# Axial attention on one core: scores interleaved as pairs of sequences, relative parts with sequences innermost, a second output bank, and another order of products

## What is computed

```
rel = arange(H)[:, None] - arange(H)[None, :] + H - 1
q_pos, k_pos, v_pos = pos_relative[:, rel]            # 4, 4 and 8 rows
qk = einsum('nhcp,nhci->nhpi', q, k)
qr = einsum('nhcp,cpi->nhpi', q, q_pos) * gate_qr
kr = einsum('nhcp,cpi->nhpi', k, k_pos) * gate_kr
att = bn(concat([qk, qr, kr])); att = att summed over the three parts
att = softmax(att, axis=-1)
att_v  = einsum('nhpi,nhci->nhcp', att, v * gate_v)
att_vp = einsum('nhpi,cpi->nhcp', att, v_pos * gate_v_pos)
z = bn(concat([att_v, att_vp])), summed over the two parts
```

## Time and profile before

| | before |
|---|---|
| median of 3 runs | 19744.31 us |
| the profiled execution | 19778.58 us, its span 19776.8 us |
| busy, whole span | PE 11295.5, DVE 10181.0, ACT 5464.1, POOL 9546.2 us |
| mean granted TensorE clock (share of 2.4 GHz) | 0.688 |
| attention stage | 2264 to 6536 us of the span |
| attention stage, busy | PE 3135.53, DVE 2030.81, ACT 1336.88, POOL 267.64 us |
| split_qk stage | 1540 to 2216 us of the span |

### The profile page before, as it was taken

One profiled execution on the slowest core, in us unless ns is written; L12 is line 12 of the kernel. 1 busy time (PEld: TensorE's weight loads), 2 busy tenths in 40 slices (PEclk: granted clock), 3 DMA queues, 4 the chain that ended last, 5 costly groups with the idle time before them and its releaser, 6 DMA issues. The chain is left out here.

```text
span 19776.8 us, 195767 instructions
## 1 busy us (share of the span) xinstructions
PE 11295.5 (57%) x62482; PEld 5033.8 (25%) x62482; DVE 10181.0 (51%) x14908; ACT 5464.1 (28%) x7509; POOL 9546.2 (48%) x8283
## 2 busy tenths in 40 slices
PE   5553477777777103332333233333347899999998
PEld 2551244444444001111111111111112233333333
DVE  4557544444444333443444344344432577777777
ACT  1114333333333000000000000000000477777776
POOL 0113200000000106886888688688820477777777
PEclk9555565656656556666656666666679999999999
DMA  4004322222222494335333533533333202021211
GB/s 95 27 27 99 61 36 39 37 37 39 37 39 36 143 194 110 94 95 131 95 94 96 130 95 94 131 94 94 94 88 71 43 20 47 20 45 22 43 22 30
DMA packets 1429876, 1407.11 MB, mean 71 GB/s; under 512 B 777265, under 2 KB 1170753, under 8 KB 1413761
## 3 DMA queue, kind: packets, MB, share of 16 engines
q1 hardware_dynamic: 1137088, 743.01, 18.5%
q0 software_dynamic: 221184, 604.27, 10.6%
q10 hardware_dynamic: 70976, 50.83, 0.8%
HBM read 1036.88 MB, written 276.84 MB: 66 GB/s over the span
## 5 line engine op out<-in xcount | busy, mean ns | idle before, releaser
L1374 POOL DMA_INDIRECT dc_g<-corners,dc_idx x4608 | 5287.7, 1148 | 1325.8 <-issue 1255.1
L1990 POOL TENSOR_TENSOR df_sq<-df_sq 128x512 f32<-128x512 f32 x1920 | 2519.3, 1324 | 1944.7 <-ACT df_sq L1938 1898.9
L1447 PE MATMUL dc_ps<-ident,dc_s 128*128 128x128 f32 x2560 | 673.8, 429 | 4339.5 <-DVE dc_s L1538 4323.9
L2085 DVE SCALAR_TENSOR_TENSOR df_pr<-df_pk,vecs,df_h 128x512 f32<-128x512 f32 x2880 | 2093.8, 742 | 610.6 <-PE df_pk L1879 343.3
L1530 DVE TENSOR_TENSOR dc_g<-dc_g,dc_wt 128x2304 f32<-128x2304 f32 x512 | 1308.9, 2556 | 1795.5 <-DMA dc_g<-corners,dc_idx 1795.4
L1938 ACT ACTIVATE df_sq<-df_pk,vecs 128x512 f32<-128x512 f32 x2880 | 1935.3, 685 | 978.6 <-DVE df_pr L2085 955.0
L748 POOL TENSOR_TENSOR at_md<-at_mt,at_own 64x512 bf16<-64x512 f32 x256 | 267.6, 1045 | 4013.8 <-DVE at_mt L938 4013.8
L920 DVE SCALAR_TENSOR_TENSOR at_x<-at_pq,hconst,at_x 128x512 f32<-128x512 f32 x1024 | 741.3, 745 | 2191.3 <-PE at_pq L785 1657.6
L1407 ACT ACTIVATE dc_st<-dc_ps 128x512 f32<-128x512 f32 x640 | 327.1, 609 | 4735.9 <-PE dc_ps L1447 4728.1
L1447 PEld LDWEIGHTS dc_ps<-ident,dc_s 128*128 128x128 f32 x2560 | 471.6, 218 | 4523.5 <-DVE dc_s L1538 3145.9
L1876 PE MATMUL df_pk<-df_t,df_wp 64*128 64x512 f32 x3840 | 1351.1, 640 | 210.4 <-ACT df_sq L1938 156.7
(11 more groups left out here) (271 smaller groups left out, 17474.2 us busy)
## 6 DMA issues: line engine op xcount, KB each, us to landing
df_h<-df_h SPq DMA_DIRECT2D x160, 512.0 KB, 7.1
dc_g<-corners,dc_idx POOLq DMA_INDIRECT x4608
corners<-dc_xt SPq DMA_DIRECT2D x16, 4160.0 KB
at_a<-y SPq DMA_DIRECT2D x192, 192.0 KB
dc_xp<-x SPq DMA_DIRECT2D x8, 4096.0 KB
cv_xp<-x SPq DMA_DIRECT2D x8, 4096.0 KB, 52.5
y<-sp_p SPq DMA_DIRECT2D x128, 192.0 KB, 2.8
y<-sp_p SPq DMA_DIRECT2D x64, 384.0 KB, 4.3
```

The lines of the kernel that those rows point to most:

```text
L1374: nc.gpsimd.indirect_dma_start(gt[:, r, k, :, :].rearrange("p a c -> p (a c)"), None, image, bass.IndirectOffsetOnAxis(ap=idx[:, s, r, k:k ...
L1447: i = nc.tensor.transpose(ps[:, j, 128 * r:128 * r + 128], sm[:, r % 2, 128 * j:128 * j + 128], env.ident[:, :])
L1990: nc.gpsimd.tensor_tensor(a, a, sq[:, (KK * n + other) % RING, :], ALU.add).then_inc(nadded, 1)
L2085: nc.vector.scalar_tensor_tensor(out=rows(pr[:, j % RING, :]), in0=rows(pk[:, j % BANKS, :]), scalar=env.vecs[:, bias:bias + 1], in1=shift ...
```

## The change

All of it lies in split_qk and attention.

- X becomes `[nh pair, p, nh of the pair]`: two nh are interleaved, so that for each position two floats lie side by side. `qk` writes every second float of its bank, `times_v` reads every second float of X, and `times_vpos` reads pairs of floats.
- `y2` and `at_a` are stored with position parity e first, then position, then the 8 sequences innermost. A relative matmul now covers positions p and p + 1 (p even), the second copy of `at_rel` is shifted by 1 instead of 64, and the matmul reads runs of 8 bf16. split_qk's second scale reads `sp_z` with stride to write this order.
- `at_pvv` has two banks; the transposed maxima lose their own bank `at_ps` and go into a bank of `at_pt`. `times_v` takes bank q % 2, `times_vpos` alternates.
- The exponential is taken in two halves (128 x 1024 each).
- TensorE's order: the products with v stand between the spreads, the next group's first `qk` comes ahead of the relative matmuls, and these are spread over all four groups, two of them already in group 0 ahead of `times_vpos`.

The diff, cut to its core:

```diff
@@ split_qk, VectorE
-                                halves = lambda v: v.rearrange("c (w e h) -> c e w h", w=8, e=2) if a else v
+                                from_z = z[:, s, :].rearrange("c (w h e) -> c e h w", w=8, e=2) if a else z[:, s, :]
...
@@ attention
-        a = sb("at_a", [128, 2, 2, HEADS, NSEQ, H // 2], BF16)
+        a = sb("at_a", [128, 2, 2, HEADS, H // 2, NSEQ], BF16)
-        X = sb("at_x", [128, 2, NH, H])
+        X = sb("at_x", [128, 2, NH // 2, H, 2])
-        pq, ptt, prr, pvv, pss = pp("at_pq", 2), pp("at_pt", 2), pp("at_prr", 2), pp("at_pvv", 1), pp("at_ps", 1)
+        pq, ptt, prr, pvv = pp("at_pq", 2), pp("at_pt", 2), pp("at_prr", 2), pp("at_pvv", 2)
@@ qk
-                        last = nc.tensor.matmul(pq[:, t % 2, 128 * e:128 * e + 128], kb[96:120, s, nh // NSEQ, c],
+                        last = nc.tensor.matmul(pq[:, t % 2, :].rearrange("p (n b e) -> p n b e", n=2, e=2)[:, e // 2, :, e % 2], kb[96:120, s, nh // NSEQ, c],
@@ transposed_maxima
-                    pe.wait_ge(mt_out, u)
-                nc.tensor.matmul(pss[0:64, 0, 0:128], mx[:, q % 2, :], env.ident[:, :], start=True, stop=True).then_inc(mt_done, 1)
+                    pe.wait_ge(subbed, 4 * u - 1)
+                nc.tensor.matmul(ptt[0:64, q % 2, 0:128], mx[:, q % 2, :], env.ident[:, :], start=True, stop=True).then_inc(mt_done, 1)
@@ times_v
-                                            X[:, s, nh, :], start=True, stop=True, tile_position=(0, 32 * j))
+                                            X[:, s, nh // 2, :, nh % 2], start=True, stop=True, tile_position=(0, 32 * j))
@@ times_vpos
-                                                X[:, s, :, p], start=True, stop=True, tile_position=(0, 32 * j))
+                                                X[:, s, :, p, :], start=True, stop=True, tile_position=(0, 32 * j))
@@ relative
-                    p = 4 * r + i
+                    p = 8 * r + 2 * i
-                                            a[0:96, s, :, :, :, p].rearrange("c e h n -> c e (h n)"), start=True, stop=True)
+                                            a[0:96, s, :, :, p // 2, :].rearrange("c e h n -> c (e h) n"), start=True, stop=True)
@@ TensorE, work
-            RELS = {1: ((0, 1, 2), (3, 4)), 2: ((5, 6, 7), (8, 9)), 3: ((10, 11, 12), (13, 14, 15))}
+            RELS = {0: ((0, 1),), 1: ((2, 3), (4, 5, 6)), 2: ((7,), (8, 9, 10, 11)), 3: ((12,), (13, 14, 15))}
...
+                    spread_next(0)
+                    spread_next(1)
                     qk(k, s, q, (2, 3))
+                    times_v_next((0, 1))
+                    spread_next(2)
+                    times_v_next((2, 3))
+                    spread_next(3)
+                    if q < 3:
+                        qk(k, s, q + 1, (0, 1))
+                    elif not final:
+                        qk(k + 1, 1 - s, 0, (0, 1))
                     for part in range(2):
+                        if not final and part < len(RELS[q]):
+                            for r in RELS[q][part]:
+                                relative(k + 1, 1 - s, r)
                         if q == 0 and not first:
                             for f in (2 * part, 2 * part + 1):
-                                times_vpos(k - 1, 1 - s, f, lambda: pe.wait_ge(av_out, 4 * k - 1))
+                                positional(k - 1, 1 - s, f, 1 - f % 2, False)
...
                         if part == 0:
                             transposed_maxima(k, s, q)
@@ ScalarE
-                nc.scalar.activation(X[:, s, :, :].rearrange("p n (e q) -> p n e q", e=2)[:, :, :, 4 * r:4 * r + 4],
-                                     prr[:, r % 2, :].rearrange("p (a e n) -> p n e a", a=4, e=2), ACT.Copy).then_inc(rel_out, 1)
+                nc.scalar.activation(X[:, s, :, 8 * r:8 * r + 8, :], prr[:, r % 2, :].rearrange("p (q n e) -> p n q e", q=8, e=2),
+                                     ACT.Copy).then_inc(rel_out, 1)
...
-                g = X[:, s, 16 * q:16 * q + 16, :]
-                nc.scalar.activation(g, g, ACT.Exp).then_inc(exped, 1)
+                for i in range(2):
+                    act.wait_ge(subbed, 16 * k + 4 * q + 2 * i + 2)
+                    g = X[:, s, 8 * q + 4 * i:8 * q + 4 * i + 4, :, :]
+                    nc.scalar.activation(g, g, ACT.Exp).then_inc(exped, 1)
-            RELS = {1: range(0, 5), 2: range(5, 10), 3: range(10, 16)}
+            RELS = {1: range(0, 5), 2: range(5, 11), 3: range(11, 16)}
```

More of the change, by code:

```diff
@@ L818, in times_v, with times_vpos @@
                     at = ((nh % NSEQ) * HEADS + nh // NSEQ) * 9
[L819 to L820 removed]
+                    last = nc.tensor.matmul(pvv[32 * j:32 * j + 9, q % 2, 128 * t:128 * t + 128], vt[:, s, at:at + 9],
+                                            X[:, s, nh // 2, :, nh % 2], start=True, stop=True, tile_position=(0, 32 * j))
                 if t == 3:
                     last.then_inc(av_done, 1)
[L824 removed]
+            def times_vpos(k, s, f, bank, free):
                 if f == 0:
[L827 to L830, removed]
+                    pe.wait_ge(exped, 8 * k + 8)
+                free()
                 for i in range(8):
@@ L856, in work, with spread_next, times_v_next @@
                     older = (k, s, q - 2) if q >= 2 else (k - 1, 1 - s, q + 2)
-                    for t in range(2):
+                    def spread_next(t):
                         if not (first and q == 0):
                             spread(*prev, t)
-                    qk(k, s, q, (2, 3))
-                    for t in range(2, 4):
-                        if not (first and q == 0):
-                            spread(*prev, t)
-                    if not (first and q < 2):
-                        if q == 1:
-                            before = lambda: pe.wait_ge(vp_out, 4 * (k - 1) + 4)
-                        elif first and q == 2:
-                            before = lambda: None
-                        else:
-                            before = lambda: pe.wait_ge(av_out, 4 * k + q - 2)
-                        for t in range(4):
-                            times_v(*older, t, before)
+                    def times_v_next(ts):
+                        if first and q < 2:
+                            return
+                        if first:
+                            free = lambda: None
+                        elif q == 0:
+                            free = lambda: pe.wait_ge(av_out, 4 * k - 3)
+                        elif q == 3:
+                            free = lambda: pe.wait_ge(av_out, 4 * k)
+                        else:
+                            free = lambda: pe.wait_ge(vp_out, 4 * k + q - 2)
+                        for t in ts:
+                            times_v(*older, t, free)
@@ L875, in work @@
                         if q == 0 and not first:
                             for f in (2 * part, 2 * part + 1):
-                                times_vpos(k - 1, 1 - s, f, lambda: pe.wait_ge(av_out, 4 * k - 1))
-                        if q and not final:
-                            for r in RELS[q][part]:
-                                relative(k + 1, 1 - s, r)
+                                positional(k - 1, 1 - s, f, 1 - f % 2, False)
                         if part == 0:
-                            if q < 3:
-                                qk(k, s, q + 1, (0, 1))
-                            elif not final:
-                                qk(k + 1, 1 - s, 0, (0, 1))
```

55 lines of the change are left out of this document (30 added, 25 removed).

## The result

| | before | after |
|---|---|---|
| median | 19742.9 us (4 runs) | 19289.4 us (19270.0 to 19296.6, 4 runs) |
| ratio | 1 | 0.9769, 95% interval 0.9752 to 0.9786 |
| the profiled execution | 19778.58 us | 19283.13 us, its span 19281.3 |

The change takes off 454 us, 7.1 us for each of the 64 blocks. I had forecast 10.1, and 19095 us.

What follows compares the result with a forecast made beforehand. The prediction saw no saturated engine but a loop of waits: groups of 18.9 + 10.6 + 11.95 + 14.45 = 55.9 us a block against 66.04, 649 us over 64 blocks, giving 19095 us; range 18850 to 19440.

Steps and rivals of the forecast that it cites:

- Group structure: Attention loop, spread to spread at 1.2 GHz: group 1 10.6 us, group 2 11.95, group 3 14.45, group 0 18.9.
- Relative matmuls from 0.96 to 0.48 a group: TensorE's relative groups of four matmuls, reading runs of 8, priced like `qk`: 0.48 us instead of 0.96.
- The wait for the load: Group 0: TensorE, ready at 6.6 us, stands still 4.7 us until the next block's load lands at 11.3.
- A `qk` matmul stays at 0.12 us: `qk` writing every second float of its bank: 0.12 us a matmul, taken from bounds of 0.12 and 0.24.
- the 1.2 that I had named as a sign of being wrong: Sign against the forecast: eight `qk` matmuls taking over 1.2 us.
- `qk` at 0.24: Rival, chance 0.22: strided `qk` writes take 0.24 us a matmul, costing 1.3 to 1.8 us a block, 19190 us.
- v_pos passes at 1.83 and, at full clock, 1.06: Group 0's `times_vpos` passes, reading pairs, priced like `times_v`: 1.83 us at 1.2 GHz, 1.06 at 2.4, instead of 2.50.
- Group 3 and group 0 together: Attention loop: group 3 forecast at 14.45 us and group 0, with the wait for the load, at 18.9.
- The sum: All four groups: 55.9 us a block against 66.04, 10.1 saved, times 64 blocks 649 us.
- split_qk at nothing: split_qk's strided second scale: 1.14 us in place of 0.80, hidden behind ScalarE's copy, so 0 taken.
- the 150 us of its bound: split_qk's second scale at 4.88 us, a strided line's time with GpSimd beside it: 150 us.

Runs made afterwards that it cites:

- experiment 1: The change, but each score matmul writes 128 floats in a row and VectorE's addition reads the bank with a stride; ratio to the kernel before 0.9717.
- experiment 2: The change with relative groups 0 and 1 of the next block moved behind group 0's last v_pos pass; ratio to the kernel before 0.9655.
- Experiment 5: The change with the v_pos table copied once by VectorE so a matmul's eight weights lie in a row; ratio to the kernel before 0.9759.
- experiment 6: The change, but each v_pos matmul reads 64 floats in a row (other data) in place of 32 pairs; ratio to the kernel before 0.9721.
- experiment 7: The change with pairs undone: X as before, contiguous score writes and times_v reads, single floats for v_pos; ratio to the kernel before 0.9782.
- experiment 10: The change with pairs undone and group 0's two relative groups behind the last v_pos pass; ratio to the kernel before 0.9654.

## Why the prediction was right, and where it was short

- **Group structure**: right, each group somewhat longer. In the block shown groups 1 and 2 came to 11.40 and 12.61 us against 10.6 and 11.95, group 3 to 14.96 against 14.45. Over all blocks the excess over the forecast is 0.3 us in group 1, 0.6 in group 2, 0.9 in group 3 (where the loop's end adds some, which the wait for the load gives back in group 0) and 1.5 in group 0, 3.3 together; the mean block of before is 0.3 longer than the one I read, which leaves the 3. With the score writes contiguous group 2 is 11.98 (experiment 1).
- **Relative matmuls from 0.96 to 0.48 a group**: right, 0.47.
- **The wait for the load**: right in kind, and shown to be on the path by experiment 2. Its size, 4.43 us in this block and 3.5 on average against 4.7, came near by luck, since two errors worked against each other. The load arrives 12.65 us into group 0, not 11.3: it was issued 3.06 us into group 3, not 2.17, and TensorE went on 24.55 us after that, not 23.6. And TensorE is ready at 8.2, not 6.6, for its `qk` is slower. The transfers themselves took as long as forecast: the last packet ends 23.5 us after the first issue here, and 23.8 in the trace of before. What I had left out is the time from there to TensorE's start, 1.07 us here and 0.8 to 1.1 in every block.
- **A `qk` matmul stays at 0.12 us**: wrong, and the term that failed most clearly. It takes 0.23 at half clock, where eight take 1.82, over the 1.2 that I had named as a sign of being wrong, and 0.12 at full clock (eight take 0.98 us from start to start at 4071.91; with contiguous writes 0.55 at the same place, at 4016.98 in experiment 1). This was the rival *`qk` at 0.24*, priced at 1.3 to 1.8 us a block; experiment 1 measured 1.6. My reason, that strided rows jump over whole runs and this jumps over one float, was no evidence. The Trainium skill ("PSUM — Partial Sum Buffer", Specifications) said that any non-contiguous pattern significantly slows matmuls, and the runs bear it out, with a factor of 1.9 at half clock and 1.8 at full clock. The later load issue is the same error seen again: SyncE waits for that `qk`, and with contiguous writes it issues 0.85 us earlier.
- **v_pos passes at 1.83 and, at full clock, 1.06**: the first half right (1.96), the second wrong (1.87 in this block, 1.74 as the median). Pricing a read of pairs like `times_v` took the price of a read that follows the clock for one that its pattern holds back. Even half of the old 2.50, for half as many places, would have been 1.25, more than the 1.06 I took. Experiment 5 excludes the weights, experiment 6 shows the read to be the cause, worth 1.5 us a block.
- **Group 3 and group 0 together**: forecast 33.35 us, measured 36.83 in the block shown (4034.55 to 4071.38) and 35.7 on average. In that block the difference of 3.48 is 0.89 (issue) + 0.95 (from the first issue to TensorE's start) + 0.26 (first two passes) + 1.62 (last two), less 0.24 for switches and small terms.
- **The sum**: 201 us of the stage's forecast gain are missing (649 less 448). Experiments 1 and 6 give back 103 and 95 us by themselves: 198. They were not run together, and other terms (the microsecond behind the load, TensorE's readiness for it) are off too, so that this comes out so exactly is luck. What the experiments show is that each of these two terms costs about 100 us.
- **split_qk at nothing**: near enough. How the 150 us of its bound came from 4.88 the prediction does not show. Line 586, before and after:

```profile
L586 DVE TENSOR_SCALAR sp_v<-sp_z,ab x128: 798/802/806, 1542.9 to 2197.3; 64x1024 f32<-64x1024 f32 x128
```
```profile
L586 DVE TENSOR_SCALAR sp_v<-sp_z,ab x128: 802/1016/1368, 1545.6 to 2203.2; 64x1024 f32<-64x1024 f32 x128
```

The strided scale takes up to 1.37 us (I took 1.14), and the last one starts 3 us later, counted from the first.

By parts, from the experiments: relative 0.84% alone, the second bank 0.73% and the halves 0.32% when taken out, pairs nothing. They needn't add up. What the order of TensorE's work alone is worth, the part on which the forecast of the groups rests, was not tried; that it brings the rest of the 2.31% is argued from the groups' lengths and not shown.

## What to carry to other kernels

Before moving work forward, ask what it waits for: the two relative groups cost 1.1% where they stood ahead of work that needed no load; behind it TensorE no longer waited for the load. When a layout needs a stride somewhere, try it in VectorE's read of the bank before the matmul's output: here the first cost nothing and the second 0.52%. A price that holds at 1.2 GHz need not hold at 2.4 GHz when the pattern of the operand may be the limit: look for a row of the same access pattern at the higher clock, or keep the lower speed as the likelier value. And read more than one block: here group 0 alone lies between 17 and 22 us.

## What was not expected of the hardware

**Reading pairs slows the other engines.** In after, once a block, while the last two passes read pairs at full clock:

```profile
4067.95 3.34 DVE L935 SCALAR_TENSOR_TENSOR at_x<-at_pq,hconst,at_x 128x512 f32<-128x512 f32 x1
4068.11 2.36 POOL L748 TENSOR_TENSOR at_md<-at_mt,at_own 64x512 bf16<-64x512 f32 x1 [18.65 <-DVE at_mt L953]
4069.78 1.12 ACT L1005 ACTIVATE at_o<-at_pvv 128x512 f32<-128x512 f32 x1 [2.05 <-PE at_pvv L833]
```

The same three operations take 0.73, 1.04 and 0.60 us with contiguous reads (experiment 6) and 0.73, 1.06 and 0.60 with single floats (experiment 7), at the same place and clock. With contiguous weights and pairs they are still slow: 2.58, 2.12 and 0.96 (experiment 5). So it is the read of pairs. At half clock ScalarE's copy beside the same passes keeps its 0.60 us, but VectorE is slowed there too, as the maxima of experiment 2 show, which fall beside the first two passes (granted clock 0.50):

```profile
4012.20 4.82 DVE L948 TRANSPOSE_TENSOR_REDUCE at_mx<-at_x 128x16 f32<-128x512 f32 x4
```

Elsewhere four of them take 2.48 us, and beside passes that read single floats (experiment 10) each keeps its 0.67. The slow operations cost nothing in the change, since GpSimd's place ended at 4070.47 and TensorE was busy until 4071.3. Why three engines slow down at once stays open: one with which the passes compete for the same memory would fit, but no run tests that.

**A pair is not enough for full speed.** At full clock a pass of 2048 columns takes 0.96 us with contiguous reads, 1.7 to 1.95 with pairs, 2.4 with single floats 128 apart. The Trainium skill ("SBUF — State Buffer", Specifications) asks for two hits on each 16-byte line for full bandwidth, which a pair of float32 gives, and says that each step to a new line pays a penalty. At 1.2 GHz the traces show nearly the full rate for pairs (3.92 against 3.55 for two passes); at 2.4 GHz they do not (3.74 against 1.91), so two hits were not enough there.
